# A joined network kernel on one core: four small experts kept on the chip and picked by a register, shorter steps before the exponentials, and matmuls of ones in TensorE's waits

## What is computed

```python
x = x + _L0_gnn_ref(_layernorm(x), edge_index, edge_attr, ...)  # 3 rounds of messages, then 8 heads of attention
x = x + _L0_ffn_ref(_layernorm(x)[None], ...)[0]                # 8 experts, 2 picked per token, hidden 1536
x = x + _L1_gnn_ref(_layernorm(x), edge_index, ...)             # graph attention: 8 heads of 128, then 1 of 768
x = x + _L1_ffn_ref(_layernorm(x)[None], ...)[0]                # 4 experts, 1 picked per token, hidden 384

# graph attention, per head and edge
e = leaky_relu(a_src[src] + a_dst[dst], 0.2); m = segment_max(e, dst)
ex = exp(e - m[dst]); alpha = ex / (segment_sum(ex, dst)[dst] + 1e-16)
# second mixture
top = argmax(x @ Wg + bg)
y = gelu(x @ W1[top] + b1[top]) @ W2[top] + b2[top]
```

## Time and profile before

| | us |
|---|---|
| median of 3 runs (1388.77 to 1390.92) | 1389.2 |
| the profiled execution | 1389.16 |
| its span | 1387.6 |
| TensorE busy | 1248.7 (90%) |
| VectorE busy | 922.2 (66%) |
| ScalarE busy | 579.5 (42%) |
| GpSimd busy | 128.2 (9%) |

### The profile page before, as it was taken

The page is one execution under the profiler, slowest core; times in us unless marked ns, Lnnn a source line. Parts: engine busy times, 40 slices in busy tenths (PEclk is TensorE's granted clock), DMA queues, the critical chain, the costliest instruction groups (busy, mean ns, idle before and its releaser), DMA issues.

```text
span 1387.6 us, 18218 instructions
## 1 busy us (share of the span) xinstructions
PE 1248.7 (90%) x6471; PEld 1064.3 (77%) x6471; DVE 922.2 (66%) x1782; ACT 579.5 (42%) x1012; POOL 128.2 (9%) x123
## 2 busy tenths in 40 slices
PE   5999999999999899998779999999986967878876
PEld 3577569979979796666779999999985757775643
DVE  4478573374374474555749999999997689647313
ACT  2011232342332423335228888988881175221110
POOL 0000200000000000013120000000002057100101
PEclk9999999999999999998789999999997989988799
DMA  9420290500500700040466999999995100020286
GB/s 335 158 91 30 85 325 1 189 28 1 213 4 16 301 4 0 1 158 2 148 225 252 379 400 388 385 392 396 383 350 193 43 28 1 1 80 1 93 297 246
DMA packets 82907, 229.72 MB, mean 166 GB/s; under 512 B 5216, under 2 KB 18592, under 8 KB 82720
## 3 DMA queue, kind: packets, MB, share of 16 engines
q1 hardware_dynamic: 74944, 191.96, 37.5%
q0 software_dynamic: 7904, 36.97, 7.2%
HBM read 202.18 MB, written 26.74 MB: 165 GB/s over the span
## 4 chain that ended last, share of the span: by engine, by line
PE 74%; DVE 16%; DMA 4%; issue 3%; ACT 2%; SPq 0%; POOL 0%; ACTq 0%; DVEq 0%; POOLq 0%
PE dve_ps L738 11%; PE dve_ps L740 11%; PE dve_ps L739 11%; PE act_ps L738 4%; PE act_ps L739 4%; PE act_ps L740 4%; PE dve_ps L781 4%; PE dve_ps L827 3%; DMA slot<-in_e1w 2%; PE dve_ps L971 2%; PE act_ps L954 2%; PE act_ps L778 2%; PE act_ps L827 1%; PE dve_ps L1213 1%; DVE part_slot L2119 1%
## 5 line engine op out<-in xcount | busy, mean ns | idle before, releaser
L2110 DVE TENSOR_TENSOR part_slot<-slot,item_hi 128x768 fp32r<-128x768 f32 x150 | 133.0, 946 | 0.3
L1551 ACT ACTIVATE item_hi<-slot 128x768 fp32r<-128x768 f32 x156 | 118.0, 833 | 25.5 <-DMA slot<-in_e0w 20.3
L2119 DVE TENSOR_TENSOR part_slot<-slot,item_hi 128x768 fp32r<-128x768 f32 x132 | 116.5, 950 | 0.8 <-ACT item_hi L1559 0.2
L1559 ACT ACTIVATE item_hi<-slot 128x768 fp32r<-128x768 f32 x132 | 99.2, 832 | 12.4 <-DMA slot<-in_e0w 12.4
L738 PE MATMUL dve_ps<-item_hi,x_hi 128*128 128x384 f32 x288 | 100.6, 349 | 3.6 <-DVE part_slot L2110 2.3
L738 PE MATMUL act_ps<-item_hi,hid_hi 128*128 128x384 f32 x288 | 99.6, 346 | 4.0 <-DVE hid_lo L2311 4.0
L740 PE MATMUL dve_ps<-item_hi,x_lo 128*128 128x384 f32 x288 | 98.4, 342 | 0.0
L739 PE MATMUL act_ps<-part_slot,hid_hi 128*128 128x384 f32 x288 | 98.3, 341 | 0.0
L740 PE MATMUL act_ps<-item_hi,hid_lo 128*128 128x384 f32 x288 | 97.5, 339 | 0.0
L739 PE MATMUL dve_ps<-part_slot,x_hi 128*128 128x384 f32 x288 | 97.1, 337 | 0.0
L1442 ACT ACTIVATE h_t<-act_ps,par 128x256 f32<-128x256 f32 x36 | 21.1, 586 | 121.5 <-PE act_ps L845 121.5
(11 more groups left out here) (403 smaller groups left out, 3218.2 us busy)
## 6 DMA issues: line engine op xcount, KB each, us to landing
slot<-in_e0w SPq DMA_DIRECT2D x48, 2304.0 KB, 10.3
slot<-in_w SPq DMA_DIRECT2D x9, 2304.0 KB, 9.7
slot<-in_e1w SPq DMA_DIRECT2D x12, 1152.0 KB, 6.3
ea_raw<-in_edge SPq DMA_DIRECT2D x8, 1024.0 KB, 5.4
slot<-in_wqkv SPq DMA_DIRECT2D x3, 2304.0 KB, 14.7
xs<-zrow POOLq DMA_DIRECT2D x2, 3072.0 KB, 15.7
ys<-item_y POOLq DMA_DIRECT2D x16, 384.0 KB, 7.0
slot<-in_gw SPq DMA_DIRECT2D x4, 1536.0 KB, 8.7
```

The lines of the kernel that those rows point to most:

```text
L1551: go(item_hi[j][k][:, :], slot[s][:, k * D:(k + 1) * D], ACT.Copy).then_inc(up_high[j], 1)
L1559: go(item_hi[j][k][:, :], slot[s][:, k * D:(k + 1) * D], ACT.Copy).then_inc(down_high[j], 1)
L2110: vv.tensor_tensor(part_slot[s][:, ks], slot[s][:, ks], item_hi[j][k][:, :].bitcast(F32), ALU.subtract).then_inc(up_low[j], 1)
L2119: vv.tensor_tensor(part_slot[s][:, ks], slot[s][:, ks], item_hi[j][k][:, :].bitcast(F32), ALU.subtract).then_inc(down_low[j], 1)
```

## The change

1. **Second mixture.** `run_items` becomes `narrow_items`. SP loads up and down weights of all four experts in eight transfers (9.4 MB) into `experts`, an array laid over the four weight slots, as soon as the second graph layer's product has left them. TensorE reads the item's expert from `plan_i` into a register twice per iteration and addresses `experts` by it. Its order becomes: transpose this item's hidden rows, up product of the next item, transpose the rows of the item after next, down product of this item. The loaders left are the item's rows (SP) and bias row (GpSimd).
2. **Matmuls of ones.** `spend(bank, n)` issues n fp32 matmuls of `ones` by `ones` (128x128) into a PSUM bank that is free. They stand ahead of some of TensorE's waits: 26 ahead of the v product, 10 and 16 in the last two attention heads, and others in both gates, around the first two items and the last item of the first mixture, the graph heads, and before the last rows; some 285 in all.
3. **Graph heads, VectorE.** The three 128x4 steps become four 128x1 steps set between the masked maxima and four 128x1 steps behind them.
4. **Graph heads, ScalarE and GpSimd.** The table load stands ahead of the h1 copies, the eight copies to `part_slot` come one after each head's exponentials, and the low parts follow from head 2 on, the last three after head 7.
5. The mask's transposes are moved ahead of the wait for the last rows; semaphores are renamed where `Run` lost its counting functions.

```diff
@@ second mixture, SP
+            def load_expert(run, j):
+                up, down = experts[:, j * 4608:j * 4608 + DC * HALF], experts[:, j * 4608 + DC * HALF:(j + 1) * 4608]
+                sp.dma_start(up.rearrange("p (k n) -> p k n", k=DC), kview(run.up[j])).then_inc(expert_in[j], 16)
+                sp.dma_start(down.rearrange("p (k n) -> p k n", k=run.blocks), kview(run.down[j])).then_inc(expert_in[j], 16)
...
-                with sp.Fori(1, last) as k:
-                    load_x(k + 1)
-                    next_up = expert(k + 1)
-                    sp.wait_ge(run.to_dve, v + 1 + run.n_up)
-                    up_of(run, next_up, 0)
-                    sp.wait_ge(run.to_dve, run.dve_after(k))
-                    down_of(run, expert(k), 0, run.down_slots[0])
+                with sp.Fori(1, last) as i:
+                    sp.wait_ge(row_turned, 2 * (i + 2))
+                    load_x(i + 2)
...
             sp.wait_ge(sig.to_act, ACT0["gat2"])
-            up_of(run1, 0, 0)
-            down_of(run1, 0, 0, run1.down_slots[0])
-            run_items(run1)
+            for j in range(NE1):
+                load_expert(run1, j)
+            narrow_items(run1)
@@ TensorE
+            def spend(bank, n):
+                for _ in range(n):
+                    mm(bank[:, 0:P], ones[:, :], ones[:, :], start=True, stop=True)
...
+            spend(dve_ps[0], 26)
...
             def turn_probs(i):
+                if i >= NH - 2:
+                    spend(act_bank(HEAD_UNIT[f"turn_a{i}"], a0), (10, 16)[i - NH + 2])
...
+                    spend(act_ps[2 * t % RING], ((0, 12), (9, 7))[run.layer][t - 2])
+                pe.wait_ge(normed, before + t + 1)
...
             def rank_tokens(run):
+                spend(act_ps[3], (14, 6)[run.layer])
...
+                def expert(i):
+                    return pe.value_load(plan_i[0:1, bass.ds(i, 1)], min_val=0, max_val=run.ne - 1) if not (isinstance(i, int) and i == 0) else 0
+
+                def times_up(i):
+                    e = expert(i)
+                    pe.wait_ge(turned_kept, 2 * (i + 1))
+                    for k in range(DC):
+                        done = mm(up_bank[:, 0:HALF], item_xt[:, k, :], experts[:, bass.ds(e * 4608 + k * HALF, HALF)],
+                                  start=(k == 0), stop=(k == DC - 1))
+                    done.then_inc(up_done, 1)
...
+                def times_down(i):
+                    e = expert(i)
+                    wait(pe, y_ready, 2 * i)
+                    pe.wait_ge(wide_bent, i + 1)
...
                 def iteration(k):
-                    turn_x(k + 1, a, v)
-                    turn_hidden(v if isinstance(k, int) else v - 2)
-                    times_up(k + 1, a, v)
-                    times_down(k, a + 1 + run.n_turn, (v + 2, v + 3) if run.n_up > 1 else (v, v))
+                    turn_wide(k)
+                    times_up(k + 1)
+                    turn_row(k + 2)
+                    times_down(k)
...
+                spend(act_ps[0], {0: 11, 1: 8, GH - 1: 9, GH: 20}.get(g, 0))
                 for t in range(NT):
                     pe.wait_ge(g_exp, NT * g + t + 1)
@@ ScalarE
+            go(table[:, 0:1], ident[:, 0:1], ACT.Exp)
             for t in range(NT):
                 bank = bank_of(t, ACT0["h1"])
...
-            go(table[:, 0:1], ident[:, 0:1], ACT.Exp)
-            for k in range(GD // P):
+
+            def high_second_layer(k):
                 ks = slice(k % 4 * D, (k % 4 + 1) * D)
                 go(part_slot[k // 4][:, ks], slot[2 + k // 4][:, ks], ACT.Copy).then_inc(w_high, 1)
...
             for g in range(GH):
                 graph_exps(g)
+                high_second_layer(g)
@@ VectorE, graph_front
+                def raise_max(t):
+                    dve.wait_ge(g_masked, NT * g + t + 1)
+                    return vv.tensor_scalar(gdec[:, b, 1, t:t + 1], gmax[:, b, t:t + 1], a_dst[:, t:t + 1], 0.0, ALU.add, ALU.max)
...
+                    if t:
+                        then(raise_max(t - 1))
...
-                vv.scalar_tensor_tensor(gdec[:, b, 0, :], gmax[:, b, :], 0.2 * FLOOR, a_dst, ALU.max, ALU.add).then_inc(sig.dve_freed, 1)
-                then(vv.scalar_tensor_tensor(gdec[:, b, 1, :], gdec[:, b, 0, :], 5.0, gdec[:, b, 0, :], ALU.mult, ALU.max))
-                vv.tensor_tensor(gdec[:, b, 2, :], a_dst, gdec[:, b, 1, :], ALU.subtract).then_inc(g_dec, 1)
+                for t in range(NT):
+                    last = vv.tensor_scalar(gdec[:, b, 2, t:t + 1], gdec[:, b, 1, t:t + 1], -4.0, gmax[:, b, t:t + 1], ALU.mult, ALU.subtract)
@@ GpSimd
-                if g < GD // P:
+                for k in {2: (0,), 3: (1,), 4: (2,), 5: (3,), 6: (4,), 7: (5, 6, 7)}.get(g, ()):
```

More of the change, by code:

```diff
@@ L296, in build @@
         gp_t = over("gp_t", [P, 2, NT, N], 18496)
[L298 removed]
+        unread_sum = [over(f"unread_sum{j}", [P, D], D * j) for j in range(2)]
         part_dst = over("part_dst", [P, 2, NT, GH], 22592)
@@ L315, in __init__ @@
                 self.dve_freed = sem(f"dve_freed_{part}")
-        class Run(Signals):
-            def __init__(self, layer, ne, hidden, picks, up, down, scattered, results, b1, b2, up_slots, down_slots, down_banks, sel_banks,
-                         pick_banks):
-                if down_banks is not None:
-                    super().__init__(f"run{layer}")
+        class Run:
+            def __init__(self, layer, ne, hidden, picks, up, down, scattered, results, b1, b2, up_slots, down_slots, sel_banks, pick_banks):
                 self.layer, self.ne, self.picks, self.up, self.down = layer, ne, picks, up, down
@@ L1174, in turn_x @@
                         pe.wait_ge(run.x_in, 16 * (i - 1))
-                    wait(pe, run.act_freed, a)
-                    wait(pe, run.dve_freed, v if isinstance(v, int) else v - 2)
-                    for half, (bank, signal) in enumerate(((act_ps[3], run.to_act), (dve_ps[2], run.to_dve))):
+                    wait(pe, turned_kept, 2 * i)
+                    for half, bank in enumerate(row_banks):
                         for j in range(3):
                             c = 3 * half + j
-                            last = nc.tensor.transpose(bank[:, j * P:(j + 1) * P], item_x[:, c * P:(c + 1) * P], ident[:, :])
-                        last.then_inc(signal, 1)
@@ L1204, in times_down, with turn_wide @@
-                def times_down(i, a_turned, v_banks, slots=run.down_slots, ahead=1):
-                    pe.wait_ge(run.act_freed, a_turned)
-                    for s in slots:
-                        pe.wait_ge(run.w_in[s], 16 * (i + ahead))
+                            turned = nc.tensor.transpose(bank[:, j * P:(j + 1) * P], item_x[:, c * P:(c + 1) * P], ident[:, :])
+                        turned.then_inc(row_turned, 1)
+                def turn_wide(i):
+                    pe.wait_ge(wide_taken, i + 1)
+                    for j in range(run.blocks):
+                        turned = nc.tensor.transpose(wide_bank[:, j * P:(j + 1) * P], hid[:, j * P:(j + 1) * P], ident[:, :])
+                    turned.then_inc(wide_turned, 1)
@@ L1215, in times_down @@
                                       start=(k == 0), stop=(k == run.blocks - 1))
-                        last.then_inc(run.to_dve, 1)
+                        done.then_inc(down_done, 1)
+                for j in range(NE1):
+                    pe.wait_ge(expert_in[j], 32)
                 pick_rows(run, 0, xn3_hi, xn3_lo)
-                turn_x(0, 0, 0)
-                times_up(0, 0, 0)
+                turn_row(0)
+                times_up(0)
                 pick_rows(run, 1, xn3_hi, xn3_lo)
+                turn_row(1)
@@ L2377, in run_items, with add_last @@
                 last = dve.value_load(plan_i[0:1, 16:17], min_val=run.items_min - 1, max_val=run.items_max - 1)
+                hidden(0)
+                x_in(1)
                 share_last(run)
-                hidden(0)
-                def result_after(k, halves):
-                    result(run.dve_after(k) + 1 + run.n_up, k, halves)
-                def iteration(k, first=False):
-                    v = run.dve_after(k)
-                    if not first:
-                        result_after(k - 1, (1,))
-                    x_in(v)
-                    hidden(v)
-                    result_after(k, (0,))
-                iteration(0, True)
+                iteration(0)
                 with dve.Fori(1, last) as k:
                     iteration(k)
-                result_after(last - 1, (1,))
-                return last, lambda: result(run.dve_after(last), last)
-            def add_last(run, last, t, half):
+                return lambda: result(last)
+            def add_last(t, half):
                 u = 2 * t + half
-                v = run.dve_after(last) + 2
-                dve.wait_ge(run.to_dve, v + u + 1)
+                dve.wait_ge(rows_ready, 8 + u + 1)
                 part = xres[:, t, half * HALF:(half + 1) * HALF]
```

(4 more changed lines are left out.)

204 lines of the change are left out of this document (98 added, 106 removed).

## The result

The changed kernel took 1347.45 us (median of 4 runs, 1346.06 to 1351.21), the kernel before 1388.99 beside it (4 runs). The ratio is 0.9708, 95% interval 0.968 to 0.9735: 41 us faster, where 47 were forecast. The profiled execution took 1348.07 us, with a span of 1346.5 against 1387.6. Measured again beside three other kernels (experiment 1) the ratio was 0.9710.

A forecast was written before the change was run, and what follows sets the result against it. TensorE ended the chain for 74%, VectorE for 16%, DMA for 4%. Savings of 23 (clock), 12.6 (graph heads) and 11.4 (second mixture), 47.0 in all, took 1389.2 to 1342 us, range 1330 to 1368.

The forecast's parts named there:

- Second mixture: Weights on the chip make its loop TensorE's work alone, period 11.58 to 8.8 us; 11.4 us saved.
- the bias row's loop: Second mixture: store, load and landing of the bias row plus results take 6.95 us, under the 8.8 us period.
- Rival 4: Second mixture: register loads not covered (+7), or bias row's loop takes 10.5 against 8.8 (+8): 1350 us; chance 0.14.
- Graph heads, the front: VectorE's 128x1 steps shorten the front from 5.19 to 3.8 us in seven of eight heads: 9.8 us saved.
- rival 1: Graph heads: the 128x1 steps are blocked by GpSimd too, front about 8.5 us: 1379 us; chance 0.10.
- rival 2: Graph heads: each of eight 128x1 steps waits a whole GpSimd addition or low part: 1411 us; chance 0.05.
- one tensor in SBUF is free: Graph heads: by "two inputs" alone, new steps with one SBUF tensor do not wait for GpSimd; 1.35 us for eight.
- Graph heads, the start: Ahead of head 0, exponentials start with the first maximum (2.7 us), and head 1's front is no longer late (1.0).
- Graph heads, the ones: Nine matmuls of ones behind the last wait on the weights cost 0.9 us not covered.
- The clock part: Ones keep TensorE active through waits, removing low-clock dips: 25.5 us summed over stages, less a tenth, 23.
- last gate: Gate of the second mixture: 13.4 us of logits, counting, picking and transposes at half clock; 46%, 6.2 us, saved.
- Rival 3: The clock does not hold under the matmuls of ones, so 23 us are lost: 1365 us; chance 0.10.

The follow-up runs named there:

- experiment 1: Changed kernel without any matmuls of ones: 1357.66 us, ratio 0.9771; repeated 1358.77, 0.9786, beside the changed kernel itself, 1346.33, 0.9710.
- experiment 5: Changed kernel with the register load ahead of each up product of the second mixture made five times instead of once: 1352.76 us.
- Experiment 2: Changed kernel with the three 128x4 steps of before back in each graph head, in place of eight 128x1 steps: 1354.9 us, ratio 0.9758.
- experiment 6: Changed kernel with ScalarE's and GpSimd's order of before in the graph heads: 1349.66 us, ratio 0.9738.
- experiment 4: Kernel before with the second mixture's part alone, no ones, all else as before: 1373.34 us, ratio 0.9898.
- ones_trimmed: `ones_earlier` without the last graph head's nine ones and with 10 instead of 14 ahead of the first gate's counting: 1336.92 us, ratio 0.9642.
- experiment 8: Changed kernel with each matmul of ones cut from 128 moving columns to 4: 1382.19 us, ratio 0.9944.
- experiment 3: Changed kernel with four more tensor_scalar steps, on 1, 2, 3 and 4 maxima, in every graph head's front: 1368.02 us.
- ones_earlier: Changed kernel with graph head 1's eight ones replaced by 17 ahead of the wait, and 14 instead of 7 in the last gate: 1339.2 us, ratio 0.9663.

## Why the prediction was right, and where it fell short

The time lay in the range and the direction was the forecast one; it saved 41 us where I took 47.

- **Second mixture**: 11.4 taken, 12.2 measured, by the steps named: 8.73 us a period for 8.8, loads of registers hidden (experiment 5), the bias row's loop of 6.95 below the period, since the row landed 3.9 us after its issue where it had taken 7.1 (medians), and the last result 5.84 us late as before. The 2 us that I set aside for the end were too many. Rival 4 is out.
- **Graph heads, the front**: the 128x1 steps did not wait for GpSimd, so rivals 1 and 2 are out. The probe shows how near they were: steps of two elements would have waited, and the argument "one tensor in SBUF is free" that the term also rested on is false (128x2 to 128x4 wait). The steps took 0.20 to 0.22 us and started some 0.12 apart; the period came to 7.51 for 7.7. Experiment 2 gives 8.6 us for 9.8.
- **Graph heads, the start**: 3.7 taken, 1.8 to 2.8 by experiment 6.
- **Graph heads, the ones**: this term was mis-sized. I charged 0.9 us "not covered" for the nine of the last head and nothing for the eight of head 1. Both stand behind a wait that had already let TensorE idle. Measured, the ones cost 5.2 and 3.4 us in the heads in the two pairs of profiles with and without them. Without ones the heads gave 14.8 and 12.0 us, around the 13.5 of the first two terms; with them 9.6 and 8.6 where 12.6 was forecast.
- **The clock part**: 23 taken; 12.4 measured by the medians of experiment 1, 14.0 and 18.0 by its two pairs of profiles, the heads' loss included. By place, kernel before against changed kernel, with the term before the tenth in brackets: up to the first gate's transposes 4.9 us (5.35), though 1.7 of these come from a dip at 172 us in the profile of the kernel before, where no ones were set; the first gate to item 0's rows 6.6 (6.8); the first mixture behind it 0.6 (2.55); features 1.2 (1.4); second layer to its gate 3.0 (3.2); last gate 2.6 (6.2). So the step that failed most is the last gate, where I assumed that the clock holds if TensorE is kept active: TensorE was busy all of 1259 to 1270 us and was granted 0.53. Why the clock fell there stays open, since it fell in `ones_trimmed` too, with ones that filled the wait. In the first gate the clock fell for some 3 us (0.93 in the window above) and cost next to nothing, for it did so mostly under the ones. The first mixture's term is of the size by which two executions differ: the same stretch was 1.5 us shorter in the second profile of the changed kernel. What I missed in kind is that the dips are not the same in each execution: in all three profiles without ones (experiments 1 and 4) head 6's transposes ran at full clock, and in two of them most of head 7's products did.
- Rival 3, that the ones do not hold the clock, was half true: right for thin products and, in most profiles, for the last gate; wrong for 128 columns ahead of a wait in the v product, the attention heads and the first gate.
- The sums: the low end of the range is said to be half of what I took off and the heads' upper bound, which is 1.3 + 5.4 = 6.7 us and gives 1335, not 1330. The saved periods and waits of the second mixture less the 2 us are 11.5, not 11.4. Neither changes a reading.

The range, 1330 to 1368, was wide enough to hold these misses, so the time alone says little for the clock part, of which 12.4 to 18.0 came instead of 23.

Not settled: why an execution meets a dip of one length or another at 635 to 645 us. Nor was it tried whether ones between the logits would hold the clock in the gates.

## What to carry to other kernels

A filler of TensorE earned something here only ahead of a wait, in a bank that is free, with a length near the wait's; behind the wait it was added to the path, at half the clock (3.78 us for eight), and one that starts while the clock is low can run over its wait (5.92 us for 14, against 3.37). On VectorE, beside a busy GpSimd, count the elements per partition of small steps: eight steps of one element beat three of four by 8.6 us in eight heads. Weights that all fit on the chip were worth loading once and picking by register (12.2 us in six items), since the loads of registers hid behind queued products. Compare several executions before a dip of the clock is counted as a price.

## What the runs showed of the hardware that was not expected

- A TensorE that the profile shows 100% busy was granted 0.51 to 0.54 of the clock with products of 4 moving columns (experiment 8).
- A one-input `tensor_scalar` waited for GpSimd's addition from two elements per partition on, three included: 361, 1194 and 1190 ns for 2, 3 and 4 against 150 for 1 (experiment 3).
- Five register loads on TensorE cost nothing behind queued products, and left a gap of 2.85 us where its queue was empty (0.40 with one load).
- The same program without ones ran the stretch from 640 to 645 us at 0.51 in one execution and at 1.00 in another, after the clock had fallen at about 635 us in both.
- With the same 14 ones ahead of the last gate's last tile, `ones_earlier` was at full clock there and `ones_trimmed` at 0.66 (1244 to 1259 us).
